# Moving the FP4 weight pieces of the first chunk, and transposing each of them once

## The reference

```python
# s: conv, recurrence and feed-forward
x1 = pointwise(depthwise_causal_conv3(rmsnorm(xn))) + xn
x2 = min_gru(rmsnorm(x1)) + x1            # h_t = (1 - z_t) h_{t-1} + z_t * cand_t
s  = w2 @ gelu(w1 @ rmsnorm(x2) + b1) + b2 + x2
# g: gated FP4 feed-forward
h = silu(q(xn) @ q(w_gate).T) * (q(xn) @ q(w_up).T)    # 704 hidden
g = silu(q(h) @ q(w_down).T)
```

## Time and profile before

| | |
|---|---|
| median of 3 runs | 1051.51 us |
| profiled execution, its time | 1053.21 us |
| its span, first to last instruction | 1051.4 us |
| TensorE busy | 98% |
| VectorE busy | 93% |
| ScalarE busy | 60% |
| GpSimd busy | 12% |
| mean granted clock | 0.998 |

### The profile page before, as it was taken

The page is one execution under the profiler, slowest core; times in us unless marked ns, Lnnn a source line. Parts: engine busy times, 40 slices in busy tenths (PEclk is TensorE's granted clock), DMA queues, the critical chain, the costliest instruction groups (busy, mean ns, idle before and its releaser), DMA issues.

```text
span 1051.4 us, 18362 instructions
## 1 busy us (share of the span) xinstructions
PE 1031.5 (98%) x6836; PEld 960.0 (91%) x6836; DVE 973.5 (93%) x1883; ACT 627.7 (60%) x1010; POOL 123.5 (12%) x116
## 2 busy tenths in 40 slices
PE   6899999999999999999999999999999999999998
PEld 5589989999899999989999998999989999998998
DVE  7889999999999999999999999999999999999886
ACT  5766374565746557484655848456574745657452
POOL 1110211011011100111110011111101110111000
PEclk9999999999999999999999999999999999999999
DMA  7000020010102001020100102001010200101002
GB/s 255 1 21 1 1 61 1 22 41 19 44 1 61 2 22 41 2 61 1 35 27 21 41 1 61 1 22 41 22 41 1 62 1 22 41 1 41 1 2 60
DMA packets 29382, 31.45 MB, mean 30 GB/s; under 512 B 1136, under 2 KB 28528, under 8 KB 29296
## 3 DMA queue, kind: packets, MB, share of 16 engines
q1 hardware_dynamic: 28192, 29.17, 9.0%
q10 hardware_dynamic: 1104, 1.13, 0.3%
HBM read 21.90 MB, written 8.39 MB: 29 GB/s over the span
## 4 chain that ended last, share of the span: by engine, by line
PE 93%; DVE 4%; ACT 1%; issue 1%; DMA 1%; POOL 0%; ACTq 0%; DVEq 0%
PE gu_ps L1074 49%; PE w_ps L1074 30%; PE w_ps L1148 4%; PE w_ps L1097 1%; PE w_ps L1086 1%; PE gu_ps L1086 1%; PE w_ps L1197 1%; PE gu_ps L1140 1%; PE w_ps L1160 1%; PE gu_ps L1132 1%; PE w_ps L1159 1%; PE w_ps L1132 1%; PE w_ps L1140 1%; DMA ident<-identity_dram 1%; PE w_ps L1224 0%
## 5 line engine op out<-in xcount | busy, mean ns | idle before, releaser
L1074 PE MATMUL gu_ps<-gu_hi,xq_hi 128*128 128x352 f32 x512 | 167.8, 328 | 0.2 <-ACT act L896 0.2
L1074 PE MATMUL gu_ps<-gu_lo,xq_hi 128*128 128x352 f32 x512 | 165.7, 324 | 0.0
L1074 PE MATMUL gu_ps<-gu_hi,xq_lo 128*128 128x352 f32 x512 | 165.4, 323 | 0.0
L1074 PE MATMUL w_ps<-w_hi,act_hi 128*128 128x256 f32 x480 | 138.8, 289 | 0.2 <-DVE act_lo L488 0.2
L1074 PE MATMUL w_ps<-w_hi,act_lo 128*128 128x256 f32 x480 | 135.2, 282 | 0.0
L1074 PE MATMUL w_ps<-w_lo,act_hi 128*128 128x256 f32 x480 | 134.9, 281 | 0.0
L753 POOL TENSOR_TENSOR inv_rms<-ss_row,neg_half 128x4 f32<-128x4 f32 x32 | 36.2, 1130 | 682.6 <-DVE ss_row L511 682.6
L1074 PE MATMUL gu_ps<-xs_hi,w_hi 128*128 128x512 f32 x256 | 101.7, 397 | 0.0
L1074 PE MATMUL gu_ps<-xs_hi,w_lo 128*128 128x512 f32 x256 | 101.4, 396 | 0.0
L1074 PE MATMUL gu_ps<-xs_lo,w_hi 128*128 128x512 f32 x256 | 101.4, 396 | 0.0
L1074 PEld LDWEIGHTS gu_ps<-gu_hi,xq_hi 128*128 128x128 f32 x512 | 96.2, 188 | 0.5 <-issue 0.4
(11 more groups left out here) (156 smaller groups left out, 2692.5 us busy)
## 6 DMA issues: line engine op xcount, KB each, us to landing
x_res<-x_dram SPq DMA_DIRECT2D x16, 512.0 KB, 4.7
x_in<-x_dram SPq DMA_DIRECT2D x15, 512.0 KB, 3.9
out_dram<-o SPq DMA_DIRECT2D x15, 512.0 KB, 3.2
act<-w_t_dram SPq DMA_DIRECT2D x1, 1024.0 KB, 11.6
w_f<-w_t_dram SPq DMA_DIRECT2D x1, 1024.0 KB, 14.1
w_f<-w_down_dram SPq DMA_DIRECT2D x1, 704.0 KB, 9.7
hid<-w_gate_dram SPq DMA_DIRECT2D x1, 640.0 KB, 5.9
hid<-w_up_dram SPq DMA_DIRECT2D x1, 640.0 KB, 8.2
```

The source lines that it names most:

```text
L1074: done = M.matmul(psum, l, r, start=first and i == 0, stop=last and i == len(terms) - 1)
```

## The change

Only the first chunk's programs and the weights' helpers change. On VectorE the taps and y_low go ahead of the codes and values of xq; piece 0 is spread around the first norm, piece 1 comes behind it, piece 2 is spread around the second norm in place of piece 3, and piece 3 follows behind scaled_low(1). On ScalarE the casts and the parts of the pieces are reordered, and `high_weights` can do one half. On TensorE `weight_columns` is no longer called in `weight_rest`, nor `down_columns` in `down_rest`: the product with minus identity is added onto the transposes made before. pointwise_rows, the remainders, the pieces and the counts of keep_busy (14 to 16, 8 to 3) change place or size, and pieces 2 to 5 are done between ff1's tiles.

```diff
--- before.py
+++ after.py
@@ -600,27 +600,27 @@
                 ratios = front_fp4_ratios(0)
                 dve.wait_ge(pwhi_ready, 1)
                 V.tensor_tensor(pw_lo[:], pw_f, pw_hi[:].bitcast(F32), ALU.subtract).then_inc(pwlo_ready, 1)
-                rounded = fp4_round(T * NBD, ratios)
                 front_taps(0)
-                front_fp4_values(0, rounded)
                 front_y_low(0)
-                weight_values(0, weight_round(0, weight_ratios(0, weight_scales(0))))
-                scales = weight_scales(1, lambda: add_squares(0))
+                front_fp4_values(0, fp4_round(T * NBD, ratios))
+                scales = weight_scales(0)
+                add_squares(0)
+                ratios = weight_ratios(0, scales)
                 clamp_sums(0, gu_ps[:, 0, 1, :])
+                weight_values(0, weight_round(0, ratios))
+                scales = weight_scales(1, lambda: scaled(0, x1, w_ps[:, 1, :], (x1_ready, KD)))
+                scaled_low(0)
+                front_fp4_low(0)
                 weight_values(1, weight_round(1, weight_ratios(1, scales)))
-                scaled(0, x1, w_ps[:, 1, :], (x1_ready, KD))
-                scales = weight_scales(2, lambda: scaled_low(0))
-                front_fp4_low(0)
-                weight_values(2, weight_round(2, weight_ratios(2, scales)))
                 recurrence(0, 0)
                 recurrence(0, 1)
-                scales = weight_scales(3, lambda: add_squares(1))
+                scales = weight_scales(2, lambda: add_squares(1))
                 clamp_sums(1, gu_ps[:, 0, 0, :])
-                rounded = weight_round(3, weight_ratios(3, scales))
+                rounded = weight_round(2, weight_ratios(2, scales))
                 scaled(1, x1, gu_ps[:, 0, 1, :], (x2_ready, KD))
-                weight_values(3, rounded)
                 scaled_low(1)
-                for p in (4, 5):
+                weight_values(2, rounded)
+                for p in (3, 4, 5):
                     weight_values(p, weight_round(p, weight_ratios(p, weight_scales(p))))
                 down_weight(0)
                 front_moments(front_stats(1))
@@ -904,10 +904,10 @@
                     A.activation(src[:, k, :], src[:, k, :], ACT.Copy,
                                  scale=gains[:, 1 + j, k:k + 1]).then_inc(wscaled, 1)
 
-            def high_weights(j):
+            def high_weights(j, halves=range(KD)):
 
                 load, src, hi, _ = split_weights[j]
-                for k in range(KD):
+                for k in halves:
                     act.wait_ge(*((wscaled, KD * j + k + 1) if j < 2 else (load, 16)))
                     A.copy(hi[:, k, :], src[:, k, :]).then_inc(whi_ready, 1)
 
@@ -948,46 +948,47 @@
                 act.wait_ge(small_ready, 1)
                 front_y(0)
                 scaled_weights(0)
+                front_y_high(0)
                 high_weights(0)
-                front_y_high(0)
-                weight_remainder(0)
-                weight_remainder(1)
                 scaled_weights(1)
                 residual_squares(0)
                 conv_residual(0)
                 front_xq(0)
+                weight_remainder(0)
+                weight_remainder(1)
                 weight_high(0)
-                high_weights(1)
+                high_weights(1, (0,))
+                high_part(0, (ff1_done, 0))
+                high_weights(1, (1,))
+                weight_low(0)
+                gate(0, 0)
+                weight_remainder(2)
+                weight_high(1)
+                gate(0, 1)
                 high_weights(2)
-                high_part(0, (ff1_done, 0))
-                weight_high(1)
-                weight_low(0)
-                weight_remainder(2)
-                gate(0, 0)
-                gate(0, 1)
+                weight_remainder(3)
                 weight_low(1)
-                weight_remainder(3)
-                weight_high(2)
-                squares(1, x2_ready, 0, x1, (0,))
-                weight_low(2)
-                weight_remainder(4)
-                squares(1, x2_ready, 0, x1, (1,))
-                for i in range(5, 9):
+                squares(1, x2_ready, 0, x1)
+                for i in range(4, 8):
                     weight_remainder(i)
                 high_part(1, (hidden_done, KD))
+                weight_remainder(8)
                 weight_remainder(9)
+                gelus(0, range(2))
+                weight_high(2)
+                gelus(0, (2,))
+                weight_low(2)
                 weight_high(3)
-                gelus(0, range(2))
+                gelus(0, (3,))
                 weight_low(3)
-                gelus(0, (2,))
+                gelus(0, (4,))
                 weight_high(4)
-                gelus(0, (3,))
+                gelus(0, (5,))
                 weight_low(4)
-                gelus(0, (4,))
+                gelus(0, (6,))
                 weight_high(5)
-                gelus(0, (5,))
+                gelus(0, (7,))
                 weight_low(5)
-                gelus(0, (6, 7))
                 biased_residual(0)
                 down_high(0)
                 silu_gate(0, 0)
@@ -1229,9 +1230,9 @@
 
                 pe.wait_ge(wq_ready, p + 1)
                 pe.wait_ge(*((wqlo_ready, p - 1) if p >= 2 else (rest_ready, p + 1)))
-                weight_columns(p, True).then_inc(wqt_done, 1)
-
-            def weight_columns(p, alone):
+                weight_columns(p).then_inc(wqt_done, 1)
+
+            def weight_columns(p):
 
                 tiles = min(2, WT - 2 * p)
                 for k in range(KD):
@@ -1240,16 +1241,16 @@
                         last = M.matmul(w_ps[:, 2 + p % 2, at:at + P],
                                         hq[:, p % 2, t * D + k * P:t * D + (k + 1) * P], ident[:],
                                         is_transpose=True, start=at == 0,
-                                        stop=alone and k == KD - 1 and t == tiles - 1)
+                                        stop=k == KD - 1 and t == tiles - 1)
                 return last
 
             def weight_rest(p):
 
                 pe.wait_ge(wqhi_ready, p + 1)
-                weight_columns(p, False)
                 places = weight_places(p, gu_hi)
                 for i, (hi, bank) in enumerate(places):
-                    last = M.matmul(bank, minus_ident, hi, start=False, stop=i == len(places) - 1)
+                    last = M.matmul(bank, minus_ident, hi, start=False, stop=i == len(places) - 1,
+                                    skip_group_check=True)
                 last.then_inc(wqm_done, 1)
 
             def down_weight(e):
@@ -1259,71 +1260,72 @@
                     pe.wait_ge(wqlo_ready, NFULL + 1)
                 else:
                     pe.wait_ge(dnlo_ready, e)
-                down_columns(e, True).then_inc(hqt_done, 1)
-
-            def down_columns(e, alone):
+                down_columns(e).then_inc(hqt_done, 1)
+
+            def down_columns(e):
 
                 for k in range(KI):
                     last = M.matmul(w_ps[:, 2 + k // 4, k % 4 * P:(k % 4 + 1) * P], hq[:, e, k * P:(k + 1) * P],
                                     ident[:], is_transpose=True, start=k % 4 == 0,
-                                    stop=alone and (k % 4 == 3 or k == KI - 1))
+                                    stop=k % 4 == 3 or k == KI - 1)
                 return last
 
             def down_rest(e):
 
                 pe.wait_ge(dnhi_ready, e + 1)
-                down_columns(e, False)
                 for k in (0, 4):
                     n = min(4, KI - k)
                     last = M.matmul(hqt_ps[:, k:k + n, :], minus_ident, dn_hi[:, k:k + n, e * P:(e + 1) * P],
-                                    start=False, stop=True)
+                                    start=False, stop=True, skip_group_check=True)
                 last.then_inc(dnm_done, 1)
 
             def first():
                 pe.wait_ge(ld_const, 32)
                 keep_busy(11, gu_ps[:, 0, 0, :])
                 front_xc(0)
-                keep_busy(14, gu_ps[:, 0, 0, :])
-                remainder(0, None)
-                remainder(1, None)
+                keep_busy(16, gu_ps[:, 0, 0, :])
+                pointwise_rows(0)
                 pe.wait_ge(pwlo_ready, 1)
-                pointwise_rows(0)
                 pointwise(0)
                 front_xq(0)
+                remainder(0, None)
+                sum_squares(0, gu_ps[:, 0, 1, :], (ld_const, 32))
+                remainder(1, None)
                 weight(0)
-                sum_squares(0, gu_ps[:, 0, 1, :], (ld_const, 32))
-                keep_busy(8, gu_ps[:, 0, 0, :])
+                keep_busy(3, gu_ps[:, 0, 0, :])
                 spread_scale(0, w_ps[:, 1, :], (x1_ready, KD))
-                weight(1)
                 weight_rest(0)
                 remainder(2, (x1_ready, KD))
                 pe.wait_ge(rest_ready, KD)
                 gru(0, 0)
```

(27 more changed lines are left out.)

## The result

The changed kernel took 1054.81 us in the median of 10 executions (1052.77 to 1056.32), the kernel before, over 10 executions with the three shown ahead of the prediction among them, 1053.06. The ratio is 1.0022, 95% interval 1.0014 to 1.0030: slower, by 1.5 to 3.2 us. I had forecast 1052.6 us (+1.1) and no measurable change as the likeliest, with 1054.6 as the upper end. The profiled execution of the changed kernel took 1054.37 us with a span of 1052.6, 1.2 longer than that of before, where the sum said 1.1. That nearness is partly luck, as the next paragraph shows: 0.6 of the 1.2 us is a later start.

The account below looks back on a forecast made before the run. The prediction took TensorE (busy 98%) as the bound unless VectorE (93%) sets the pace, the chains meeting at gate_up(0, 1, 1). Terms 0 - 0.6 + 1.7 = +1.1 us on the median 1051.51 gave 1052.6, range 1049.8 to 1054.6.

Parts of the forecast that it names:

- the extra wait at spread_scale(0): On TensorE at the first norm: weight(0) and keep_busy(3) stand ahead, so spread_scale starts 1.1 us after its input.
- hidden(0, 0) late by 1.1 to 1.3 us: On VectorE behind the second norm: three pieces, not two, stand ahead, so it starts at 75.55 instead of 74.28, +1.3 us.
- TensorE's gain turned into a gap: Ahead of gate_up(0, 1, 1): the 4 us TensorE gained end as 4.2 us idle, and it starts at 76.5 as before.
- the fall of the clock behind it and its price: Behind the gap, in dense TensorE work: a lower clock costs +1.7 us, between 0 and 2.4.
- down_rest(1)'s 0.6 us: In TensorE's dense part: the second down_rest saves its transposes, -0.6 us.
- That loss lay outside the chain that decides (VectorE's): Kernel before, from 52.2 us on: the 1.7 us of TensorE work lost to the low clock lay outside the deciding chain.
- Against the runs shown: Step to the final time: the profiled execution was 1.7 us above the median 1051.51; sum added to the median, 1052.6.
- 2.2 us leave VectorE's way to pointwise: Front on VectorE: codes (1.06 us) and values (1.13 us) of xq moved behind y_low, so pointwise starts at 18.6, not 20.60.
- the resolution: Whole kernel: a measurement tells 0.2%, 2.1 us, from no change; faster 0.14, same 0.63, slower 0.23.
- rival 3: At gru(0, 0): the clock falls earlier as well, costing up to 1.7 us more, 1054.3 us; chance 0.22.
- rival 1: At TensorE's gap ahead of gate_up(0, 1, 1): it brings no lower clock, 1050.9 us; chance 0.12.
- Rival 2: Up to gate_up(0, 1, 1): VectorE is not late and TensorE's gain is kept, 4.7 us in full, 1046.8; chance 0.13.

Follow-up runs that it names:

- e9_before_filled: The kernel before with identity products in its two idle stretches, 5 ahead of gru(0, 0) and 8 ahead of weight(3): 1051.93 us, ratio 0.9992.
- e1_fill_gap: The changed kernel with 14 identity products in TensorE's gap ahead of gate_up(0, 1, 1): 1052.80 us, ratio 1.0006.
- e0_change: The changed kernel once more, without an edit, beside the kernel before: 1054.88 us, ratio 1.0025.
- e11_front_fill: The changed kernel with spread_scale(0) ahead of weight(0), ScalarE's front reordered, and 14 identity products ahead of gate_up(0, 1, 1): 1051.61 us, ratio 0.9988.
- e3_once_in_before: The kernel before with only one part of the change, the weight pieces' transposes made once: 1051.26 us, ratio 0.9990.
- e4_change_twice: The changed kernel with the transposes of the weight pieces made twice again, as before it: 1053.73 us.

## Why the prediction was right and where it failed

**Right: both chains up to hidden(0, 0), in the profiled execution.** The front's times from pointwise to scaled(1), the extra wait at spread_scale(0), hidden(0, 0) late by 1.1 to 1.3 us, TensorE's gain turned into a gap, the fall of the clock behind it and its price (1.5 us against 1.7), and down_rest(1)'s 0.6 us all came as worked out. Span against span the sum was 1.1 and the result 1.2, but 0.58 us of the 1.2 are the later start: the change's own part was 0.6, with the clock's price 0.2 and the start of gate_up(0, 1, 1) another 0.2 us under the forecast.

**Wrong: "That loss lay outside the chain that decides (VectorE's)".** In the profiled execution of before the fall at 52 us lay on the chain that decides, TensorE's. The prediction had itself said that VectorE had 1.3 us of room and TensorE none, so of the 1.7 us that TensorE lost ahead of that point at least 1.3 had to count. e9_before_filled shows it: without the fall hidden(0, 1) comes 1.5 us sooner.

**Wrong, and what put the time outside the range: "Against the runs shown".** The profiled execution was 1.7 us above the median of three because its clock had fallen and theirs, by their level, had not: executions with the fall have a median of 1053.5, those without 1051.8. I added a difference that holds against 1053.2 to 1051.5. The right base gives 1053.21 + 1.1 = 1054.3, and the changed kernel's level at 0.998 is 1054.1 to 1055.0. Against the fall-free level the change costs about 1.0 us for VectorE's chain less down_rest(1), as e1_fill_gap shows at a held clock (1052.79 against 1051.8), and then the clock's 1.5 us (profile) to 2 us (medians) on top in nearly all its executions.

**Wrong by a term put at nothing: the first tap.** "2.2 us leave VectorE's way to pointwise" counts the codes of xq as pure gain. They had covered the wait for ScalarE's y, and without them it cost 0.64 us in e0_change's profile and 0.86 in e11_front_fill's, nothing in the profile after. What it adds to the median no run separates.

**Wrong: the resolution.** The chances took 2.1 us as the least difference that could be told from none. The measured 1.75 us in the medians, with an interval of 1.5 to 3.2, was told from none.

**Wrong in place, as far as seen: rival 3.** Six of 19 executions have a lower mean clock, 0.997. The one of them that was profiled shows a second fall, ahead of the second norm (44 to 48 us) and not ahead of gru; where the other five had theirs is not shown. The price is 1.2 us, in that profile and between the medians of the two levels (1055.2 to 1056.3 against 1054.1 to 1055.0). A fall at gru did occur in the order of before with the transposes made once (e3_once_in_before). The range ended at 1054.6, 0.2 us short of the median, since its lower base was 1.7 us too low for most executions.

**Rivals 1 and 2.** The clock fell behind the gap in both profiled executions of the changed kernel, and by their mean clock 18 of 19 executions had a fall, so rival 1 is out for these; a single wait of 1.58 us left the clock alone (e4_change_twice). The Trainium skill's example (TensorE: Matmul & The Clock Gate, "Seeing it yourself"), a fall 5.2 us after the last matmul, read as a bound as rival 1 did, would not have touched a gap of 3.52 us; the measurement decides against that reading. Its statement in "What's actually happening", that activity releases the throttle, agrees with e1_fill_gap and e9_before_filled, where products that nothing reads kept the granted clock at 1.00. Rival 2 is out altogether: TensorE kept nothing of its gain.

## What to carry to other kernels

Compare a profiled execution's time with the level of the others before you build on it, and ask which chain its disturbances lie on: a clock that fell is part of that execution, not of the kernel. Where two engines meet at one wait, count both up to it and compare: time saved on the one that comes first becomes a gap. The gap of 3.5 us on TensorE was not neutral here: it cost 1.5 us behind it, through the clock. Work moved out of small waits on one engine into a row without any lengthens that row, even if the total stays the same, and it uncovers the waits that it had filled.

## What the runs showed of the hardware

The kernel before, unchanged, has two levels 1.7 us apart, 43 and 46 of 89 executions, that go with a mean granted clock of 1.000 or 0.998; 13 identity products in two idle stretches took the upper one away. Sparing the second set of transposes of the eight weight pieces in the changed kernel made it slower by 1.15 us, because the gap in TensorE grew from 1.6 to 3.5 us and the granted clock fell to 0.50 in the dense work behind it; a wait of 1.58 us in the same place left the clock at 1.00. Eleven identity products at the start of TensorE's work took 3.99 us in one execution of the changed kernel and 4.85 in another, and the transposes behind them moved by as much.
